# Rounded down products in the first half of a shared FFN, two buffers for rounded context, and five changes of order

## The reference, cut to what matters

```python
x = x + tanh(g_xattn) * cross_attention(layernorm(x), ctx)      # 16 heads of 16, one context of 128 per 128 tokens
xf = layernorm(x)                                               # 2048 tokens of 256
logits = xf @ Wg; two of 16 experts for each token, softmax over the two
y = sum over e: (silu(xf @ W1[e] + b1[e]) * (xf @ W11[e] + b11[e]) @ W2[e] + b2[e]) * gate[e]
z = silu(xf @ Ws1 + bs1) * (xf @ Ws11 + bs11) @ Ws2 + bs2       # shared FFN, 1024 hidden
x = x + tanh(g_ffn) * (y + z)
```

## Time and profile before

| what | us |
|---|---|
| median of 3 runs | 571.85 (568.67 to 572.27) |
| the profiled execution | 574.73 |
| its span | 572.6 |
| PE busy | 546.3 (95%) |
| PE weight loads busy | 440.9 (77%) |
| DVE busy | 353.6 (62%) |
| POOL busy | 333.2 (58%) |
| ACT busy | 238.5 (42%) |
| one pair in the attention loop | 20.2 |

### The profile page before, as it was taken

The page is one execution under the profiler, slowest core; times in us unless marked ns, Lnnn a source line. Parts: engine busy times, 40 slices in busy tenths (PEclk is TensorE's granted clock), DMA queues, the critical chain, the costliest instruction groups (busy, mean ns, idle before and its releaser), DMA issues.

```text
span 572.6 us, 12049 instructions
## 1 busy us (share of the span) xinstructions
PE 546.3 (95%) x3290; PEld 440.9 (77%) x3291; DVE 353.6 (62%) x861; ACT 238.5 (42%) x788; POOL 333.2 (58%) x273
## 2 busy tenths in 40 slices
PE   7889999999979999988999999999999999999996
PEld 6556667666758878777888888888888888888785
DVE  5757788787678732345665566555665556435677
ACT  1899999999994201202222122221222212232232
POOL 4689999998863486623364674444444830236550
PEclk8999999999999999999999999999999999999999
DMA  8571001000112144335458777656665210113332
GB/s 284 245 300 64 21 20 38 29 26 20 65 39 103 46 166 174 105 98 185 140 177 293 249 287 259 201 201 211 211 211 201 82 46 29 35 54 107 109 111 73
DMA packets 32899, 76.08 MB, mean 133 GB/s; under 512 B 4961, under 2 KB 21857, under 8 KB 29921
## 3 DMA queue, kind: packets, MB, share of 16 engines
q1 hardware_dynamic: 14960, 52.44, 25.5%
q10 hardware_dynamic: 14832, 14.82, 8.0%
q0 software_dynamic: 3072, 8.39, 4.7%
HBM read 54.93 MB, written 18.61 MB: 128 GB/s over the span
## 4 chain that ended last, share of the span: by engine, by line
PE 80%; DVE 8%; issue 5%; another core or an unknown queue 3%; ACT 2%; POOL 2%; DVEq 0%; ACTq 0%; POOLq 0%
PE mid L749 14%; PE big L730 8%; PE big L731 8%; PE big L732 7%; PE big L517 5%; PE big L653 4%; PE mid L740 4%; PE big L651 3%; PE big L652 3%; PE mid L530 3%; PE work L549 3%; PE last L670 2%; PE work L670 2%; PE last L542 2%
## 5 line engine op out<-in xcount | busy, mean ns | idle before, releaser
L939 ACT ACTIVATE last<-arena 128x512 f32<-128x512 f32 x47 | 28.3, 602 | 183.3 <-DVE arena L1409 183.3
L837 ACT ACTIVATE arena<-big,nmax 128x128 f32<-128x128 f32 x256 | 90.7, 404 | 9.0 <-DVE nmax L1061 8.4
L749 PE MATMUL mid<-dring,arena 128*128 x376 | 88.9, 379 | 0.0
L1409 DVE TENSOR_TENSOR arena<-big,bring 128x512 f32<-128x512 f32 x47 | 32.5, 692 | 87.2 <-PE big L732 87.2
L730 PE MATMUL big<-u_hi,xsT_hi 128*128 x188 | 81.8, 435 | 1.6 <-issue 1.6
L1572 POOL TENSOR_TENSOR u_lo<-arena,u_hi 128x2048 fp32r<-128x2048 f32 x16 | 74.4, 4652 | 1.3
L749 PEld LDWEIGHTS mid<-dring,arena 128*128 128x128 f32 x376 | 67.8, 190 | 7.4
L732 PE MATMUL big<-u_hi,xsT_lo 128*128 x188 | 73.5, 391 | 0.0
L731 PE MATMUL big<-u_lo,xsT_hi 128*128 x188 | 73.4, 390 | 0.0
L1548 POOL TENSOR_TENSOR arena<-arena,rinv 128x1024 f32<-128x1024 f32 (+1 forms) x32 | 58.7, 1834 | 13.3 <-DVE rinv L1069 13.0
L1672 POOL TENSOR_TENSOR pool_mark<-mhalf 128x1 f32<-128x1 f32 x15 | 2.9, 194 | 104.0 <-PE big L732 87.6
(11 more groups left out here) (198 smaller groups left out, 1202.9 us busy)
## 6 DMA issues: line engine op xcount, KB each, us to landing
arena<-up_w_dram SPq DMA_DIRECT2D x16, 1024.0 KB, 7.6
bring<-expert_bias_dram SPq DMA_DIRECT2D x16, 640.0 KB
dring<-down_w_dram SPq DMA_DIRECT2D x18, 512.0 KB
sorted_y<-arena ACTq DMA_DIRECT2D x47, 128.0 KB, 1.7
arena<-sorted_x ACTq DMA_DIRECT2D x43, 128.0 KB, 2.1
sorted_x<-dring SPq DMA_DIRECT2D x3, 1536.0 KB, 9.4
arena<-ctx_t_dram ACTq DMA_DIRECT2D x8, 256.0 KB, 2.8
dring<-up_w_dram SPq DMA_DIRECT2D x2, 1024.0 KB, 4.8
```

The costliest lines, as they stand in the source:

```text
L749: i = mm(mid[:, 1, 0:D], gT[:, p, c, :], dring[:, slot, c * D:(c + 1) * D], start=(c == 0), stop=(c == HC - 1))
L837: i = nc.scalar.activation(probs[:, u % 2, h, :], big[:, u % 2, h // 4, (h % 4) * CTX:(h % 4 + 1) * CTX], ACT.Exp, bias=nmax[:, u % 2, h:h ...
L1409: v.tensor_tensor(hb1[:, p, :], big[:, p, 0, :], bring[:, slot, 0:HID], ALU.add).then_inc(h1_ready, 1)
```

## The change

- **First half of the shared FFN.** Its downs are done as in the tail: shared_down(n) works on a chunk, 12 rounded products into the four banks of first_bank. ACT rounds the chunk (round_hidden), DVE subtracts (keep_rest). The down weights get hi and lo parts, first_d, one cast on ACT and one subtraction on DVE; the chunk's parts lie in first_gs. Ups and downs alternate: up n, down n - 2 (n - 3 for the middle ones).
- The transposes of rows 0 and 1 go to big, and both come before the last down chunk; the first expert block comes after it. The counts' products go to other columns of mid, and the first down waits until they are read. The first silu of the experts waits for all 16 tiles.
- keep_xfT(LAST) goes from POOL to ACT (hi) and DVE (lo). POOL's split of item 2 waits for the last keep_rest of the first half.
- **Rounded context** gets two buffers (ctx_r, in room freed from bring); the load of the context comes one unit earlier, the hi part in unit 1, the lo part at the end of unit 3.
- **Orders.** WARM 16 instead of 10. In pair 0 POOL rounds W_k in unit 0 and subtracts in unit 1, and multiplies the output bias after normalise(0, 0); PE makes scores(1, 1) after the transposes. In the last pair the output projection comes after the transposes of unit 0. At the end up 14 and up 15 come together ahead of down 12, and both last combines follow the last subtraction.

```diff
-WARM = 10
+WARM = 16
+        ctx_r = sb("ctx_r", [P, 2, 2, DC * 2 * CTX], F32R)
...
+        first_d = sb("first_d", [P, 2, DCOLS], F32R)
+        first_gs = sb("first_gs", [P, 2, 2, 512], F32R)
...
+        first_bank = (work, last, mid[:, 0, :], mid[:, 1, :])
...
+        def rounded_chunk(n):
+            if n < HC * TILES // GROUP:
+                return first_gs[:, 0, n % 2, :], first_gs[:, 1, n % 2, :]
+            return gs_hi[:, n % 2, :], gs_lo[:, n % 2, :]
...
+                    if not behind and u == 2:
+                        scores(j + 1, 1)
+                    if not ahead and u == 0:
+                        pe.wait_ge(o_taken, 2 * j - 1)
+                        project_out(j - 1, 1)
...
-            def shared_down(s, tiles=range(GROUP)):
...
-                        i = mm(zbank[t % 2][:, 0:D], gshT[:, s % 2, c, t * P:(t + 1) * P], dring[:, slot, c * D:(c + 1) * D],
-                               start=(c == 0), stop=(c == HC - 1))
+            def shared_down(n):
+                h, c = divmod(n, HC)
...
+                pe.wait_ge(gs_lo_ready, n + 1)
+                if n == 0:
+                    pe.wait_ge(d_split, 1)
+                    pe.wait_ge(lg_taken, PAIRS)
+                    pe.wait_ge(rank_taken, 1)
...
+                for t in range(GROUP):
+                    if c == 0 and h > 0:
+                        pe.wait_ge(z_taken, GROUP * (h - 1) + t + 1)
...
+                    mm(banks[t][:, 0:D], g_hi, w_hi, start=(c == 0), stop=False)
+                    mm(banks[t][:, 0:D], g_hi, w_lo, start=False, stop=False)
+                    i = mm(banks[t][:, 0:D], g_lo, w_hi, start=False, stop=(c == HC - 1))
...
             shared_up(0, 3)
+            shared_down(0)
             pe.wait_ge(xfT_kept, 4)
...
+            for n in range(4, 8):
+                shared_up(1, n - 4)
+                shared_down(n - 3)
+            shared_down(5)
             pe.wait_ge(xfT_kept, PAIRS)
...
+            for n in range(8, 15):
+                shared_up(n // HC, n % HC)
+                shared_down(n - 2)
...
-            transpose_rows(0, 0)
-            shared_down(3, range(1))
-            transpose_rows(1, 1)
+            shared_up(3, 3)
+            shared_down(13)
+            shared_down(14)
+            transpose_rows(0, 0, big[:, 0, 0, :])
+            transpose_rows(1, 1, big[:, 0, 1, :])
+            shared_down(15)
+            pe.wait_ge(xsT_ready, 2)
+            pe.wait_ge(gsh_ready, HC * TILES // GROUP)
             up(0, 0)
-            pe.wait_ge(xsT_ready, 2)
-            shared_down(3, range(1, GROUP))
-            pe.wait_ge(z_taken, 4 * GROUP)
+            pe.wait_ge(z_taken, TILES)
             transpose_rows(2, 2)
...
+            for n in range(2, 4 * HC - 2):
                 shared_up(4 + n // HC, n % HC)
+                shared_down(TILES + n - 2)
+            shared_up(7, HC - 2)
+            shared_up(7, HC - 1)
+            shared_down(TILES + 4 * HC - 4)
+            for n in range(4 * HC - 3, 4 * HC):
+                shared_down(TILES + n)
...
+                if early:
+                    if not isinstance(j, int):
+                        act.wait_ge(ctx_split, j - ROUNDED)
+                    act.wait_ge(v_ps, j - 1)
...
+            shared_silu(0, 0)
+            act.wait_ge(w_even, 32)
+            nc.scalar.activation(first_d[:, 0, :], dring[:, 0, :], ACT.Copy).then_inc(d_hi_done, 1)
+            round_hidden(0)
+            act.wait_ge(xfT_ready, PAIRS)
+            nc.scalar.activation(xfT_hi[:, :, 2 * P * LAST:2 * P * PAIRS], xfT[:, :, :], ACT.Copy).then_inc(xfT_hi_kept, 1)
...
-                    act.wait_ge(z_taken, 4 * GROUP - 1)
+                    act.wait_ge(z_taken, 4 * GROUP)
...
+                    if behind and ahead2 and u == 1:
+                        round_context(j + 2, slot)
                     if ahead and behind and u == 2:
                         copy_v(j + 1, 1 - slot)
-                    if behind and ahead2 and u == 2:
-                        round_context(j + 2, slot)
                     if behind and u == 2:
                         copy_xfT(j - 1)
-                    if behind and ahead2 and u == 2:
-                        keep_context(j + 2, slot)
                     if behind and u == 3:
                         choose_copy(j - 1)
                         choose(j - 1)
+                    if behind and ahead2 and u == 3:
+                        keep_context(j + 2, slot)
...
+            keep_rest(0)
+            dve.wait_ge(d_hi_done, 1)
+            v.tensor_tensor(first_d[:, 1, :], dring[:, 0, :], first_d[:, 0, :], ALU.subtract).then_inc(d_split, 1)
             shared_hidden(0, [2])
...
+                if n == 4 * HC - 2:
+                    shared_hidden(4 + h, [c + 1])
...
+            keep_rest(TILES + 4 * HC - 1)
+            for t in range(TILES - 2, TILES):
+                combine(t)
             add_shared(7)
...
+                    if isinstance(j, int) and j == 0 and u == 1:
+                        split_projection(1, 0)
                     if u < UNITS - 1:
                         normalise(j, u + 1)
...
+            normalise(0, 0)
             pool.wait_ge(bo_loaded, 16)
             pool.wait_ge(tanh_ready, 1)
             g.tensor_tensor(bo_g, bo_bc, tanh_g[:, 0:1].to_broadcast([P, D]), ALU.mult).then_inc(bo_ready, 1)
-            normalise(0, 0)
...
-                if t == GROUP - 1:
-                    keep_xfT(LAST)
...
+            pool.wait_ge(gs_lo_ready, TILES)
             split(PIECES, raw[:, 0, :], 0, 0, 1)
```

More of the change, by code:

```diff
@@ L122, in flamingo_layer @@
         dring = sb("dring", [P, WSLOTS, DCOLS])
-        bring = sb("bring", [P, WSLOTS, BCOLS])
+        with nc.sbuf_tensor("bring", [P, WSLOTS, BCOLS], F32) as whole:
+            bring = whole
+        ctx_r = sb("ctx_r", [P, 2, 2, DC * 2 * CTX], F32R)
+        sb("bring_rest", [P, WSLOTS * BCOLS - 4 * DC * 2 * CTX])
         xsT_hi = sb("xsT_hi", [P, 2, D], F32R)
@@ L148, in flamingo_layer @@
         ARENA = 16128
-        arena = sb("arena", [P, ARENA])
+        with nc.sbuf_tensor("arena", [P, ARENA], F32) as whole:
+            arena = whole
+        first_d = sb("first_d", [P, 2, DCOLS], F32R)
+        first_gs = sb("first_gs", [P, 2, 2, 512], F32R)
+        sb("arena_rest", [P, ARENA - 2 * DCOLS - 4 * 512])
         taken = [0]
@@ L354, in chunk_used @@
             if c == HC - 1:
-                engine.wait_ge(z_ps, TILES + GROUP * (h + 1))
+                engine.wait_ge(z_ps, GROUP * (h + 1))
             else:
@@ L491, in project_q, with project_v @@
                     project(0, xnT, q_ps, bank)
-            def project_v(j, bank=work, halves=range(2)):
+            def project_v(j, bank=work, halves=range(2), slot=0):
                 src = ctxT_1 if isinstance(j, int) and j == 1 else ctxT
@@ L576, in pair @@
                         scores(j, u + 2)
-                    elif ahead:
+                    elif ahead and (behind or u == 2):
                         scores(j + 1, u - 2)
-                    if behind and u == 1:
-                        pe.wait_ge(kT_ready, DC * j + 2 * DC) if ahead else pe.wait_ge(o_taken, 2 * j - 1)
+                    if behind and ahead and u == 1:
+                        pe.wait_ge(kT_ready, DC * j + 2 * DC)
                         project_out(j - 1, 1)
@@ L1288, in _, with copy_rows @@
             pair(LAST, 1, False, True, False)
-            def copy_rows(b, p):
+            def copy_rows(b, p, bank=work):
                 dve.wait_ge(xs_ps, b + 1)
```

235 lines of the change are left out of this document (115 added, 120 removed).

## The result

| | median, us | runs | beside the kernel before |
|---|---|---|---|
| kernel before | 571.44 (568.12 to 573.21) | 20 | |
| changed kernel | 573.72 (570.45 to 578.20) | 20 | 1.0043, 95% interval 1.0026 to 1.0060 |
| changed kernel, profiled execution | 571.09, span 569.3 | 1 | |

The change made the kernel 0.4% slower, where 560.4 us was forecast. The two profiled executions do not show that difference: that of before (574.73 us) lies above the 20 runs of its kernel, that of after (571.09) is the second fastest of its own. Their difference, -3.6 us, is therefore no measure of the change. What they and the traces of the experiments can show is where in the kernel time is won and lost.

A forecast was written before the change was run, and what follows sets the result against it. TensorE was taken as the bound, busy 546.3 of 572.6 us. Gains of 7.0 + 1.5 + 1.5 + 1.2 + 0.3 + 0 = 11.5 us, from a median of 571.85, gave 560.4 us; range 555 to 566.5.

The forecast's parts named there:

- 1.0 for all three: Shared first half: down chunks opening a tile group wait for DVE additions, covered unless a signal is late; 1.0 us charged.
- new waits in the shared stage: Rival, chance 0.12: DVE's longer queue or late signals keep PE waiting at each chunk; 565.7 us.
- rival "slower": Chance 0.04: DVE's subtractions slow POOL's scatter issues, expert rows land late, 12.8 us are lost; 573.2 us.
- The shared stage: First shared up to third rows' transposes: rounded downs and four banks give 75.4 against 82.4 us, 7.0 less; bounds 5 and 9.5.
- The stall at the first down: Shared first half: PE reaches the first down before DVE has read the counts' bank; a new stall of 1.0 us.
- Block 1: Expert weights of item 2: POOL splits them 4.4 us later, ready at 252, wanted only after item 1's blocks.
- Rows for the first experts: Start of the experts: row loads land before PE wants them at 245.6, hidden by some 2.5 us.
- Warm-up: Kernel start: twelve more records of zero products cost nothing; 1.5 us won if the clock stays at 2.4 GHz, else 0.
- First pair: First attention pair: POOL's bias product after the normalise and W_k's rounding moved; 1.5 us less, bounds 0.5 and 2.2.
- Attention loop: Attention pairs: the context's cast moves, PE's 0.50 us xfT wait goes; 1.2 us less in all, bounds 0 and 2.0.
- Last pair: Last attention pair: output projection moves into a gap where PE waited 0.89 us for ACT; 0.3 us less, bounds 0 and 1.
- Tail: Kernel end: the last two ups together, two combines after the last subtraction; gain 0, bounds 0.6 lost and 0.9 won.

The follow-up runs named there:

- e11: The kernel before, with scatter and tail gathers issued so that a tile's wait for the landing of two tiles earlier; 566.53 us, 0.9985 beside the kernel before.
- e3: The changed kernel with 4 of the 32 scatter DMAs, so most expert rows are zero; 564.30 us, 0.9855 beside the kernel before.
- e12: The changed kernel with 10 warm-up products of zeros (WARM = 10), as before; 563.87 us, 0.9913 beside the kernel before.
- e13: The changed kernel itself, run again on another chip; 562.17 us, 0.9912 beside the kernel before.
- e14: The changed kernel with DVE's four small gate operations moved behind its work for the first two expert blocks; 560.74 us, 0.9884 beside the kernel before.
- e10: The changed kernel with later gate operations, scatter and tail gathers each waiting for the landing of two tiles earlier; 560.54 us, 0.9863 beside the kernel before.
- e7: The changed kernel itself, run once more on another chip; 568.41 us, 0.9954 beside the kernel before.

## Why the prediction was wrong, step by step

**Late signals (the step that failed).** The prediction charged "1.0 for all three" places where a down chunk opens a tile group, "unless a signal is late", and gave new waits in the shared stage 0.12 with a loss of 3.3 us there. The trace of before had the evidence: its silus of chunks 12 to 15 began 1.2, 1.4, 2.6 and 2.7 us after PE's last product, and one was 3.2 us late in the tail. PE's last products of chunks 14 and 15, and ACT's silus for them:

```profile
234.94 0.39 PE L653 MATMUL big<-xfT_hi,u_lo 128*128 128x512 f32 x1
237.78 0.39 PE L653 MATMUL big<-xfT_hi,u_lo 128*128 128x512 f32 x1
```

```profile
237.93 0.69 ACT L924 ACTIVATE arena<-big,bias 128x512 f32<-128x512 f32 x1 [3.61 <-remote]
240.84 0.69 ACT L924 ACTIVATE arena<-big,bias 128x512 f32<-128x512 f32 x1 [2.22 <-remote]
```

They cost some 2.3 us there (83.74 against e11's 81.41), and I priced them by what they cost before, not by their length in an order without slack. The one stall of the trace after is 5.07 us plus about 1.7 for the clock after it (3.4 us at half speed), 6.8 together: the 6.9 by which its shared stage is longer than e3's. The measured 573.7 us lies beside the 573.2 of the rival "slower", but by luck: that rival's slow scatter did not happen in the trace after, whose 32 issues took 46.7 us, before 46.8.

**The shared stage without them** came out right: forecast 75.4 us; by the prediction's own ends, from the first up to the third rows' transposes, it is 75.24 (e3), 75.19 (e12) and 75.63 (e13). Part of that is luck, since its terms missed both ways. PE idles 2.4 us in e3 where the four waits add up to 3.6, and its work is 1.1 us above the plain sum. The openings of the tile groups cost nothing instead of 1.0, the wait before the first expert block 1.6 instead of 1.2. The 0.4 for switching ACT's function, which no row gave, is 0 in the trace after: ACT loads its table at 252.08, for 1.28 us, and then waits 4.03 us for DVE. The stall at the first down was forecast at 1.0 and is 0.65, with DVE's counts as the releaser:

```profile
186.55 0.35 PE L701 MATMUL work<-first_d,first_gs 128*128 128x256 f32 x1 [0.65 <-DVE cnt L1398]
```

What it replaces was too high: of the 5.9 us of idling that I put down to two alternating banks, 2.3 were late signals (83.74 against 81.41 in e11). The forecast took a stage without them from one that had them. Without them in both, the gain is 4.5 us (80.12 to 75.63) and not 7.0; to block 1's ups, the column of the table, it is 5.7.

**Block 1, the next term missing.** I gave POOL's split of item 2 a start 4.4 us later in the stage, and it is 4.9 in e13 (69.1 us after the first shared up, before 64.2). But I asked only when its result is due; what mattered was what DVE does beside it: 2.7 us, in no term of the sum.

**Rows for the first experts.** "Hidden by some 2.5 us" holds in e14, where SP issues them 64.4 us after the first shared up. In e13 it is 67.0, since 11 of the 32 scatter issues took over 1.1 us and the scatter 49.1 us instead of 46.5 (before: 3 issues, 46.8). There PE just waits for the rows:

```profile
242.12 0.97 PE L747 MATMUL big<-const,arena 128*128 128x128 f32 x4 [0.18 <-DMA arena<-sorted_x]
```

That is the mechanism of the rival "slower", at 2.6 of its 15.6 us.

**Warm-up: right.** The chain of waits of after, and of e12 with 10 products:

```profile
7.16 1.73 PE work L478 x8
```

```profile
8.29 2.72 PE work L478 x8
```

First scores at 11.4 to 12.3 us with 16 products, at 13.5 to 14.1 in four of five traces with 10. In the fifth (e11) they came at 12.01 and the eight records took 1.73 too, so ten are at times enough; PE's gap behind the products of zeros was 1.08 us there, in the four others 1.48 to 2.49. The granted clock of 0.5 that was expected of e12 near 8 us cannot be read: its first clock record is at 10.17. The length of its products is what shows the half speed.

**First pair: right mechanism, half the size.** 0.76 us against 1.5 (39.27 to 38.51), the same in every trace. POOL's timeline of after shows the bias product behind normalise, and W_k's subtraction in a place where it delays the next normalise less:

```profile
17.14 1.90 POOL L1603 TENSOR_TENSOR arena<-arena,rinv 128x1024 f32<-128x1024 f32 x1 [2.80 <-DVE rinv L1104]
18.99 0.61 POOL L1696 TENSOR_TENSOR arena<-arena,tanh_g 128x256 f32<-128x256 f32 x1
...
24.97 1.27 POOL L1638 TENSOR_TENSOR u_lo<-arena,u_hi 128x512 fp32r<-128x512 f32 x1
```

**Attention loop: right.** 1.16 us against 1.2 (117.50 to 116.35). The wait for xfT shrank from 0.50 to 0.20, and copy_k's slack did not turn the gain into a loss. The subtraction did meet POOL, as the prediction feared: in the trace after it ran from 115.86 to 117.24, beside POOL's normalise from 114.80 to 116.70, and took 1.38 us where others of its shape take 0.69. It ended after POOL's, and yet the loop kept its gain, so "leave the loop nothing" did not follow. PE's wait:

```profile
111.37 0.66 PE L472 MATMUL work<-const,arena 128*128 128x128 f32 x4 [0.20 <-DVE xfT L1166]
```

**Last pair: wrong**, 0.3 against 0 at best and -1.9 with the clock's fall.

**Tail: wrong by 1.4, outside my bound of 0.6.** PE's part is the same in both orders where nothing is late, 71.20 (e11) and 71.17 (e10). Both gaps that I traded against each other, the 1.28 us before the last downs and the 1.4 behind the two ups, exist only with late signals: before has 1.28 and after 1.79, and neither e11 nor e10 has any gap above 0.1 us in its second half. Behind PE it grew from 3.68 to 5.08. DVE's timeline at the end of e10 (new order), then of e11 (old order):

```profile
551.66 0.69 DVE L1349 TENSOR_TENSOR u_lo<-arena,u_hi 128x512 fp32r<-128x512 f32 x1 [0.74 <-ACT u_hi L954]
552.27 0.48 DVE L1522 SCALAR_TENSOR_TENSOR x_all<-arena,gate,x_all 128x256 f32<-128x256 f32 x1
...
553.70 0.48 DVE L1524 SCALAR_TENSOR_TENSOR x_all<-arena,gate,x_all 128x256 f32<-128x256 f32 x1
...
555.14 1.00 DVE L1360 SCALAR_TENSOR_TENSOR x_all<-mid,tanh_g,x_all 128x256 f32<-128x256 f32 x2
```

```profile
558.58 0.69 DVE L1458 TENSOR_TENSOR u_lo<-arena,u_hi 128x512 fp32r<-128x512 f32 x1 [0.70 <-ACT u_hi L987]
559.18 0.48 DVE L1470 SCALAR_TENSOR_TENSOR x_all<-arena,gate,x_all 128x256 f32<-128x256 f32 x1
...
561.14 1.00 DVE L1320 SCALAR_TENSOR_TENSOR x_all<-mid,tanh_g,x_all 128x256 f32<-128x256 f32 x2
```

Between the last subtraction and the last four additions stand two combines instead of one, 1.8 us instead of 0.9; the other 0.5 us lies behind the last addition, where the results are stored.

**The sum without late signals**, e11 against e13: scores +0.2 (-1.3 to -1.8 against the four traces in which ten products were not enough), first pair -0.7, loop -1.2, shared stage -5.7, block 1 +2.3, after PE +1.4, together -3.7; with those four -5.2 to -5.8. The medians on the chip of e13 give -4.7. So even there the gain of 11.5 us was more than twice too large; in the first measurement it was gone altogether and 2.3 us more. Late signals cost both kernels, the changed one more: from the first measurement to the chip of e13 the median fell from 571.4 to 566.9 us before and from 573.7 to 562.2 after. These are different chips, so other differences may be in it.

**What stays open.** Why the first measurement gives 1.0043 and the chip of e7, with late signals too, 0.9954. The granted clock fits the direction: its median over the first 20 runs is 0.9925, 0.994 in e7's ten, and 1.000 in e13's five, and the two slowest of the 20 (577.5 and 578.2 us) have the two lowest values, 0.985 and 0.981. This was read, not tested by a run. Nor did I find how a scatter makes PE's signals late, and no trace of the first measurement besides the one shown was kept, though it is among the fastest of its 20; how much the late signals took from the slower ones is not shown.

## What to carry to other kernels

Before an order is tightened, read how late each signal already comes in the slack order, and price the new one by that lateness: a signal 2.7 us late that cost little before became a stall of 5.07 us in the new order, and a clock fall may follow it. Ask of every moved block of POOL work what DVE has to do in the same microseconds, not only when its result is due. And a change whose parts each win 1 us can only be judged on the same chip: here one and the same kernel stood from 0.9912 to 1.0043 beside the kernel before.

## What the runs showed of the hardware that I had not expected

- PE's semaphore updates came late while POOL issued indirect DMAs, in the first measurement and on two chips: in the trace after by up to 7.22 us, of which ACT stood ready for 5.04. The updates of ACT, DVE and POOL did not. In the ten traces of the three other chips none was late (a silu 0.04 us after its product). With 4 instead of 32 scatters PE's were on time in the first half on a chip that had late ones, and late again at that trace's gathers.
- A DVE operation of 16 columns took 2.92 us beside POOL's subtraction of 128x2048, and 0.16 away from it.
- After gaps of 1.45 and 0.42 us the clock fell to 0.50 in 7 of 14 traces of the same order, for 3.4 or 6.8 us; after three gaps of 0.9 us in none of 6.
